# Who issues the 25 fills of the second adjacency matrix, and when

## The chip, the cores and the metric

The kernel runs on one core of one Trainium2 chip. The metric is the device time of one execution in microseconds (us). The engines are TensorE (PE; its weight loads are PEld), VectorE (DVE), ScalarE (ACT), GpSimd (POOL) and the sync engine (SP). A name with a q, as SPq, is the engine's sequencer, which also issues DMAs. SP and ACT have a DMA queue each (q1 and q10), GpSimd has q0, and all of them feed the same 16 DMA engines.

## The reference

The program is a chain of eight layers over 3125 nodes with 256 features: a graph layer and a feed-forward layer, four times. The change touches what the graph layers of level 1 and level 2 need, which are two weighted sums over the same 50,000 edges:

```python
# level 1 (four times)
norm = dinv[src] * dinv[dst]
out = segment_sum(h[src] * norm[:, None], dst) + b
# level 2 (twice)
norm = dis[row] * ew * dis[col]
out = segment_sum(h[row] * norm[:, None], col) + b
```

## The kernel before, in words

The kernel turns both sums into dense matrix products. It builds two matrices of 3200 rows by 3125 columns in HBM, one cell for each pair of nodes: `count_cells` holds how many edges join the pair (used by level 1), `weight_cells` the sum of their weights (used by level 2). Each is first filled, in 25 transfers of 128 rows (1562.5 KB each), from a stripe in SBUF, `edges_stripe`, that is zero but for a diagonal of ones. Then GpSimd adds the edges in, with scatters that add: one indirect DMA takes 128 cells.

The edges come in 392 columns of 128, in 49 windows of 8 columns (`NW = 49`, `WT = 8`). A scatter may not name a cell twice, and an add may not overtake another to the same cell. So edges of one window that fall into one cell are merged first, and GpSimd waits for all scatters of a window to land before it starts the next one.

Stages of PE, ACT, DVE and SP stand in one block and are separated by a barrier of those four engines. GpSimd isn't in these barriers: its work runs beside them, in its own order, and joins only at the end of the block. The order, with the lines:

- `cells_of_edges` (L493): ids of the cells, their digits, the gather of x. ACT issues the 25 fills of `count_cells` (L562).
- `cells_and_degrees` (L765): the merge. Class `Earlier` compares the edges of a window on PE and ACT, and DVE closes each window (L747). SP loads the digits, four transfers for a window, four windows ahead (`load`, L675): `sp.wait_ge(self.scored, WT * (w - self.RING + 1))` with `RING = 4`, so SP goes on to window w when window w - 4 is scored.
- `layer0_gnn` (from L992), `layer0_ffn`, `layer1_table` (L1341): the next layers; DVE waits at L1026 for all 25 fills of `weight_cells`. The last thing that SP issues there is `bins<-zeros` (L1349), 8704 KB of zeros to HBM.
- GpSimd beside all of it: `add_windows` (L464) calls `add_window` (L444) for each of the 49 windows. It waits for all 25 fills of `count_cells` once, then for the window's cells, then for the scatters of the window before; then it issues the eight scatters (L455) and, in windows 0 to 12, two fills of `weight_cells` (L460; one in window 12). After the last window it waits for all scatters.
- The block ends when all five engines are there (L2668), the semaphores are cleared, and the next block begins: `layer1_gnn` loads `count_cells` on SP (L1400), and GpSimd begins to scatter into `weight_cells` (L874).

Of the kernel before, what the change touches and what calls it, by code (L numbers as in the profile page):

```python
# [21 lines left out]
N = 3125  # L22
T = 25
P = N // T
# [12 lines left out]
NW = ET // WT  # L37
# [203 lines left out]
def linear(nc, g, tag, src, width, w_dram, bias_dram, nout, finish, prepare=None, turn=None, table=None,  # L241
# [10 lines left out]
    with ExitStack() as ctx:  # L252
# [17 lines left out]
        @block.sync  # L270
        def _(sp):
            column_loads = 0
            with nc.allow_non_contiguous_dma("a few hundred values"):
                for k, dram in enumerate((scale_dram, shift_dram)):
                    if dram is not None:
                        sp.dma_start(columns[0:rows, k, :], dram.rearrange("(k p) -> p k", p=rows)).then_inc(c_loaded, 16)
                        column_loads += 1
            if not in_sbuf:
                sp.dma_start(w[0:rows], w_dram.rearrange("(k p) n -> p k n", p=rows)).then_inc(w_loaded, 16)
            if bias is not None:  # L280
                sp.dma_start(bias[:, :], bias_dram.partition_broadcast(128)).then_inc(b_loaded, 16)
            for load in more_loads:
                load(sp)
            if table is not None:
                out = table[0].rearrange("(p t) d -> p t d", p=P)
                for t in range(0, T, G):

                    sp.wait_ge(put_away, t + G)
                    sp.dma_start(out[:, t:t + G, :], table[1][0:P, t:t + G, 0:nout]).then_inc(stored, 16)
                sp.wait_ge(stored, 16 * (T // G))  # L290
            for loads, loaded in ((column_loads, c_loaded), (not in_sbuf, w_loaded), (bias is not None, b_loaded)):
                if loads:
                    sp.wait_ge(loaded, 16 * loads)
# [143 lines left out]

FILLS = 2  # L440
FIRST_FILLS = 6


def add_window(nc, g, pool, w, e):  # L444


    rows = g.count_cells.rearrange("r (c a) -> (r c) a", a=1)
    if w == 0:
        pool.wait_ge(g.counts_filled, 16 * T)
    pool.wait_ge(g.cells_ready, w + 1)  # L450
    if w:

        pool.wait_ge(g.counts_added, 16 * WT * w)
    for t in range(w * WT, min((w + 1) * WT, EC + 1)):
        pool.indirect_dma_start(out=rows, out_offset=bass.IndirectOffsetOnAxis(ap=g.cell_row[:, t:t + 1], axis=0),  # L455
                                in_=g.cell_count[:, t:t + 1], in_offset=None, compute_op=ALU.add
                                ).then_inc(g.counts_added, 16)

    for j in range(FILLS * w, min(FILLS * (w + 1), T)):
        pool.dma_start(g.weight_cells[j * 128:(j + 1) * 128, :],  # L460
                       e.stripe[:, e.middle - j * P:e.middle - j * P + N]).then_inc(g.weights_filled, 16)


def add_windows(nc, g, e):  # L464


    @g.block.gpsimd
    def _(pool):
        for w in range(NW):
            add_window(nc, g, pool, w, e)  # L470
        pool.wait_ge(g.counts_added, 16 * (EC + 1))
# [182 lines left out]
class Earlier:  # L654
# [20 lines left out]
    def load(self, sp):  # L675
        own, other = self.e.side
        for w in range(NW):
            if w >= self.RING:
                sp.wait_ge(self.scored, WT * (w - self.RING + 1))
            tiles = slice(w * WT, (w + 1) * WT)  # L680
            j = w % self.RING
            for side, to, lo, hi in ((own, 0, 0, 5), (own, 5, 0, 3), (other, 0, 0, 3), (other, 5, 0, 5)):
                sp.dma_start(side[to:to + hi - lo, j, :],
                             self.g.digits_dram[lo:hi, tiles, :].rearrange("r t p -> r (t p)")).then_inc(self.loaded[j], 16)

    def start(self, dve):
        nc = self.nc
        nc.vector.memset(self.nothing[:, :], 0.0)
        nc.vector.tensor_copy(self.ident[:, :], self.g.ident[:, :])
        dve.wait_ge(self.e.later_ready, 1)  # L690
        nc.vector.tensor_copy(self.later[:, :], self.e.later[:, :])
        dve.drain().then_inc(self.copied, 1)
# [188 lines left out]
def aggregate(nc, g, tag, acc, table, width, weighted=False, field=0, loads=()):  # L881
# [4 lines left out]
    with ExitStack() as ctx:  # L886
# [11 lines left out]
        @block.sync  # L898
        def _(sp):
            for k, load in enumerate(loads):  # L900

                sp.wait_ge(multiplied, R + ST * (2 * k + 1) // (2 * len(loads)))
                load(sp)
# [1817 lines left out]
```

## Time and profile before

| | |
|---|---|
| median of 3 runs | 4455.87 us (4450.1 to 4464.65) |
| the profiled execution's own time | 4456.35 us |
| its span, first to last instruction | 4454.6 us |
| mean granted TensorE clock | 0.848 of full |
| PE busy | 3212.8 us, 72% |
| GpSimd busy | 2267.1 us, 51% |
| DVE busy | 1418.9 us, 32% |
| ACT busy | 882.3 us, 20% |

The shares are means over a program with many stages, so they don't say what a change in one stage is worth. The rows below are read from the first 1040 us of the span, where the change lies.

### The profile page before, as it was taken

How to read it: one execution, taken by the hardware profiler on the slowest of the kernel's cores; microseconds unless marked ns; L12 is line 12 of the kernel's file. 1: busy time of each engine (PE TensorE's matmuls, PEld its weight loads, DVE VectorE, ACT ScalarE, POOL GpSimd, SP SyncE). 2: the span in 40 equal slices, each digit the busy share in tenths (PEclk: the TensorE clock that was granted, in tenths of full speed). 3: DMA queues.
4: the chain of work that ended last, by engine and by line, in shares of the span. 5: the costliest groups of instructions: out<-in, count | busy, mean ns of one | idle time of the engine just before them, and what ended most of it. 6: DMA issues, size and time to landing. Idle time of an engine off the chain costs nothing. (4 is left out here: it accounts for less than half of the span.)

```text
span 4454.6 us, 56530 instructions
## 1 busy us (share of the span) xinstructions
PE 3212.8 (72%) x17915; PEld 2414.4 (54%) x17916; DVE 1418.9 (32%) x3628; ACT 882.3 (20%) x2505; POOL 2267.1 (51%) x1830
## 2 busy tenths in 40 slices
PE   0999855675999982893299999788785554553893
PEld 0555443565999982893288888645332222222562
DVE  3333365442531132012612111233433443442005
ACT  0666622120000000331301100133101111111220
POOL 5587777775666666665056665300006655552003
PEclk9999967787999995996699999789896676665996
DMA  8663212229999875797144334100343222232222
GB/s 338 236 182 77 9 2 5 11 16 282 274 294 266 257 190 156 195 244 182 25 150 145 131 118 146 44 0 0 118 140 89 84 81 80 80 75 70 92 95 68
DMA packets 368073, 562.48 MB, mean 126 GB/s; under 512 B 177053, under 2 KB 246493, under 8 KB 351584
## 3 DMA queue, kind: packets, MB, share of 16 engines
q1 hardware_dynamic: 201740, 393.74, 27.6%
q0 software_dynamic: 158320, 122.06, 14.8%
q10 hardware_dynamic: 7824, 44.20, 2.4%
q8 instruction: 114, 1.87, 0.2%
q14 instruction: 75, 0.61, 0.0%
HBM read 413.40 MB, written 145.88 MB: 126 GB/s over the span
## 5 line engine op out<-in xcount | busy, mean ns | idle before, releaser
L455 POOL DMA_INDIRECT count_cells<-cells_count,added_row x391 | 647.8, 1657 | 280.9 <-issue 119.5
L919 POOL DMA_INDIRECT g3g_got<-relations,g3g_idx x416 | 394.6, 948 | 765.2 <-ACT g3g_idx L912 645.1
L874 POOL DMA_INDIRECT weight_cells<-added_weight,added_row x391 | 609.3, 1558 | 318.5 <-DMA weight_cells<-added_weight,added_row 182.1
L1435 PE MATMUL g_acc<-XN,g_blocks 125*125 125x128 f32 x5000 | 567.3, 275 | 55.3 <-DMA g_blocks<-count_cells 52.7
L932 PE MATMUL g3g_pp<-g3g_got,g3g_hot 128*125 128x256 f32 x832 | 361.5, 563 | 325.6 <-DVE g3g_hot L943 153.2
L1435 PEld LDWEIGHTS g_acc<-XN,g_blocks 125*125 125x125 f32 x5000 | 559.2, 189 | 60.0 <-issue 52.9
L1748 PE MATMUL g_acc<-g_H,g_blocks 125*125 125x256 f32 x2500 | 552.4, 380 | 20.1 <-DMA g_blocks<-weight_cells 15.3
L1665 POOL DMA_INDIRECT slots_dram<-sort_rec,sort_row x392 | 379.4, 968 | 341.3 <-issue 120.1
L1748 PEld LDWEIGHTS g_acc<-g_H,g_blocks 125*125 125x125 f32 x2500 | 470.0, 188 | 94.7 <-issue 24.0
L932 PEld LDWEIGHTS g3g_pp<-g3g_got,g3g_hot 128*125 128x125 f32 x832 | 169.5, 255 | 518.1 <-DVE g3g_hot L943 271.3
L961 DVE TENSOR_TENSOR X<-X,g3g_pp 125x256 f32 x416 | 175.3, 421 | 362.8 <-issue 305.6
L723 ACT ACTIVATE same_same<-same_scores 128x128 bf16<-128x128 f32 (+7 forms) x392 | 255.1, 651 | 145.1 <-PE same_scores L712 127.2
L708 PE MATMUL same_scores<-edges_other,edges_own 11*128 11x512 bf16 (+2 forms) x490 | 206.9, 483 | 22.5 <-ACT same_same L723 21.5
L912 ACT CAST g3g_idx<-slots 128x1 int32 x416 | 79.4, 191 | 621.8 <-PE g3g_pp L932 409.3
L1792 DVE SCALAR_TENSOR_TENSOR g_tmp<-g_acc,dinv,g_b 125x256 f32<-125x256 f32 x50 | 24.2, 484 | 495.4 <-PE g_acc L1748 378.3
L2588 POOL DMA_INDIRECT f3y_Y<-results,f_back x25 | 36.0, 1440 | 275.2 <-PEq L86 267.8
L1875 PE MATMUL g_psO<-g_w,g_xT 128*125 128x512 f32 x400 | 173.7, 595 | 0.0
L943 DVE TENSOR_SCALAR g3g_hot<-iota,slots 128x125 f32<-128x125 f32 x424 | 127.6, 302 | 56.0 <-issue 42.7
L1456 ACT ACTIVATE g_uT<-g_psT 128x125 f32<-128x125 f32 (+1 forms) x75 | 20.6, 275 | 627.3 <-PE g_psT L1410 474.8
L2145 PE MATMUL f1e_pY<-w,XN 128*128 x512 | 123.0, 384 | 10.0 <-issue 10.0
L2123 PEld LDWEIGHTS f1e_pH<-XN,f1e_w 128*128 128x128 f32 x1040 | 128.2, 194 | 3.6 <-issue 0.2
L2123 PE MATMUL f1e_pH<-XN,f1e_w 128*128 128x128 f32 x1040 | 128.5, 278 | 0.0
(625 smaller groups left out, 4658.6 us busy)
## 6 DMA issues: line engine op xcount, KB each, us to landing
g_blocks<-count_cells SPq DMA_DIRECT2D x500, 312.5 KB
g_blocks<-weight_cells SPq DMA_DIRECT2D x50, 1562.5 KB
count_cells<-edges_stripe ACTq DMA_DIRECT2D x25, 1562.5 KB
weight_cells<-edges_stripe POOLq DMA_DIRECT2D x25, 1562.5 KB
f1e_w<-in_L_ffn_w SPq DMA_DIRECT2D x68, 512.0 KB
relations<-g_ys SPq DMA_DIRECT2D x25, 896.0 KB
f_w<-in_L_ffn_w SPq DMA_DIRECT2D x16, 1024.0 KB, 8.4
bins<-zeros SPq DMA_DIRECT2D x1, 8704.0 KB, 32.7
```

What stands on the lines that cost most here:

```text
L455: pool.indirect_dma_start(out=rows, out_offset=bass.IndirectOffsetOnAxis(ap=g.cell_row[:, t:t + 1], axis=0), in_=g.cell_count[:, t:t + 1], ...
L708: nc.tensor.matmul(self.scores[:, k % self.SCORES, lo:hi], own[:, j, n:n + 128], other[:, j, lo:hi], start=True, stop=True)
L723: self.nc.scalar.activation(self.same[:, k % self.SAME, 0:n], self.scores[:, k % self.SCORES, 0:n], ACT.Relu, accum_out=self.found[:, k:k ...
L874: pool.indirect_dma_start(out=rows, out_offset=bass.IndirectOffsetOnAxis(ap=g.cell_row[:, t:t + 1], axis=0), in_=g.cell_weight[:, t:t + 1] ...
L919: pool.indirect_dma_start(out=got[:, j, :], out_offset=None, in_=table[:, :], in_offset=bass.IndirectOffsetOnAxis(ap=idx[:, j:j + 1], axis ...
L932: nc.tensor.matmul(pp[0:P, j % BANKS, 0:width], hot[:, j, :], got[:, j, :], start=True, stop=True).then_inc(multiplied, 1)
L961: nc.vector.tensor_tensor(part, part, pp[0:P, j % BANKS, 0:width], ALU.add).then_inc(added, 1)
L1435: last = nc.tensor.matmul(acc[0:P, i % ACCS, 0:128], blocks[0:P, i % BLOCKS, t * P:(t + 1) * P], rhs[p][:, t, :], start=(t == 0), stop=(t ...
L1665: pool.indirect_dma_start(out=g.slots_dram[:, :], out_offset=bass.IndirectOffsetOnAxis(ap=self.row[:, c:c + 1], axis=0), in_=self.rec[:, c ...
L1748: last = nc.tensor.matmul(acc[0:P, i % 3, 0:D], blocks[0:P, i % BLOCKS, t * P:(t + 1) * P], H[p][0:P, t, :], start=(t == 0), stop=(t == T ...
L1875: last = nc.tensor.matmul(psO[0:P, c, :], xT[:, j, k, :], w[:, k, 2 * c:2 * c + 2, :].rearrange("p r n -> p (r n)"), start=(k == 0), stop= ...
L2123: last = nc.tensor.matmul(pH[:, j % 2, f * 128:(f + 1) * 128], w1[:, j % AHEAD, k, f * 128:(f + 1) * 128], xT[:, j % 2, k * 128:(k + 1) * ...
```

## The change

The two fills behind the scatters of windows 0 to 12 are removed from GpSimd. In their place SP issues one fill behind its digit loads of every odd window (1, 3, ..., 47) and one behind those of window 48, 25 in all. Data, sizes, the semaphore and who waits for it stay.

```diff
-FILLS = 2
@@ add_window
-    for j in range(FILLS * w, min(FILLS * (w + 1), T)):
-        pool.dma_start(g.weight_cells[j * 128:(j + 1) * 128, :],
-                       e.stripe[:, e.middle - j * P:e.middle - j * P + N]).then_inc(g.weights_filled, 16)
@@ Earlier.load
             for side, to, lo, hi in ((own, 0, 0, 5), (own, 5, 0, 3), (other, 0, 0, 3), (other, 5, 0, 5)):
                 sp.dma_start(side[to:to + hi - lo, j, :],
                              self.g.digits_dram[lo:hi, tiles, :].rearrange("r t p -> r (t p)")).then_inc(self.loaded[j], 16)
+            if w % 2 == 1 or w == NW - 1:
+                t = w // 2
+                sp.dma_start(self.g.weight_cells[t * 128:(t + 1) * 128, :],
+                             self.e.stripe[:, self.e.middle - t * P:self.e.middle - t * P + N]).then_inc(self.g.weights_filled, 16)
```

## Rows read from the trace of the kernel before

**Rows 1.** Where the engines reach the end of the first block (queue instructions, line L2668)

```profile
L2668 DVEq COMPARE_BRANCH  x1: 41/41/41, 999.4 to 999.4; - x1
L2668 POOLq COMPARE_BRANCH  x1: 41/41/41, 1031.3 to 1031.3; - x1
L2668 POOLq DRAIN  x1: 4467/4467/4467, 1031.5 to 1031.5; - x1
```

**Rows 2.** All scatters of L455: ns min/median/max, first and last start; what it waited for

```profile
L455 POOL DMA_INDIRECT count_cells<-cells_count,added_row x391: 1532/1541/7094, 147.2 to 1021.9; - x196
  issue: 119.5, 344
  DMA count_cells<-cells_count,added_row: 94.2, 46
```

**Rows 3.** Timeline of GpSimd: first scatter, boundary of windows 0 and 1 (start, us)

```profile
147.15 1.62 POOL L455 DMA_INDIRECT count_cells<-cells_count,added_row  x1 [67.21 <-DMA count_cells<-edges_stripe]
...
160.67 1.54 POOL L455 DMA_INDIRECT count_cells<-cells_count,added_row  x1 [0.30 <-issue]
161.66 1.77 POOL L460 DMA_DIRECT2D weight_cells<-edges_stripe  x2
164.45 1.65 POOL L455 DMA_INDIRECT count_cells<-cells_count,added_row  x1 [1.02 <-DMA count_cells<-cells_count,added_row]
```

**Rows 4.** First scatters of windows without a fill before them, in and after the merge

```profile
414.89 1.54 POOL L455 DMA_INDIRECT count_cells<-cells_count,added_row  x1 [2.08 <-DMA count_cells<-cells_count,added_row]
...
432.35 1.54 POOL L455 DMA_INDIRECT count_cells<-cells_count,added_row  x1 [2.10 <-DMA count_cells<-cells_count,added_row]
...
537.75 1.54 POOL L455 DMA_INDIRECT count_cells<-cells_count,added_row  x1 [2.06 <-DMA count_cells<-cells_count,added_row]
...
554.27 1.54 POOL L455 DMA_INDIRECT count_cells<-cells_count,added_row  x1 [2.06 <-DMA count_cells<-cells_count,added_row]
```

**Rows 5.** The moved issues: ns min/median/max, first and last start

```profile
L460 POOL DMA_DIRECT2D weight_cells<-edges_stripe x25: 1148/1161/1187, 161.7 to 377.0; - x25
```

**Rows 6.** Stretches: PE, PEld, DVE, ACT, POOL busy, clock, DMA share, GB/s

```profile
125.00:142.00 17.00, 16.06 (x144) 9.35 (x144) 5.79 (x25) 11.34 (x31) 0.00 (x0) 1.00 1.02 424
143.00:144.00 1.00, 1.00 (x7) 0.39 (x6) 0.91 (x3) 0.80 (x3) 0.00 (x0) 1.00 0.35 146
```

**Rows 7.** Timeline of SP: digit loads of windows 2, 3, 5, 7 and 9 (first half)

```profile
113.65 2.29 SPq L683 DMA_DIRECT2D edges_own<-digits_dram  x2
...
122.92 2.26 SPq L683 DMA_DIRECT2D edges_own<-digits_dram  x2
...
129.63 1.32 SPq L683 DMA_DIRECT2D edges_own<-digits_dram  x2
131.00 2.19 SPq L683 DMA_DIRECT2D edges_other<-digits_dram  x2
...
147.17 0.56 SPq L683 DMA_DIRECT2D edges_own<-digits_dram  x2
...
164.70 1.34 SPq L683 DMA_DIRECT2D edges_own<-digits_dram  x2
```

**Rows 8.** PE's first digits; SP's last digit loads, and its next stage

```profile
113.99 0.28 PE L710 MATMUL same_scores<-edges_other,edges_own 11*128 11x128 bf16 x1 [7.63 <-DMA edges_other<-digits_dram]
...
507.21 0.59 SPq L683 DMA_DIRECT2D edges_other<-digits_dram  x2
547.75 0.42 SPq L995 DMA_DIRECT2D l0g_w<-in_L_gnn_weight  x1
```

**Rows 9.** The end of the scatters and the zero fill (timeline; stretches; the wait of L874)

```profile
998.35 0.61 SPq L1349 DMA_DIRECT2D bins<-zeros  x1
...
1010.80 1.54 POOL L455 DMA_INDIRECT count_cells<-cells_count,added_row  x1 [6.29 <-DMA count_cells<-cells_count,added_row]
...
1021.87 1.54 POOL L455 DMA_INDIRECT count_cells<-cells_count,added_row  x1 [0.30 <-issue]
...
1026.00:1028.00 2.00, 0.00 (x0) 0.00 (x0) 0.00 (x0) 0.00 (x0) 0.00 (x0) 0.50 0.51 85
...
  DMA weight_cells<-added_weight,added_row: 182.1, 47
```

## The prediction

> **What bounds the kernel now.** I read first who arrives last at the end of the first block. DVE is there at 999.4 us, GpSimd only at 1031.3 us, and its drain takes another 4.5 us [rows 1]. So for the first 1036 us it is GpSimd's list of scatters that sets the time, and the other engines have 1031.3 - 999.4 = 32 us to spare. What comes after this block (the matrix products of level 1 start from the join) is shifted by whatever GpSimd is shifted, one for one.
>
> Second, GpSimd's own list. The 391 scatters run from 147.2 to 1021.9 us at 1.54 us each; between them lie 119.5 us of issue gaps and 94.2 us of waits for the scatters of the window before; ahead of the first stands a wait for the fills of `count_cells` [rows 2, 3]. It never waits for the merge. The list has two levers: when it starts, and how long a window takes.
>
> Third, the start. GpSimd's first scatter begins at 147.15 us, released by the fills of `count_cells` [rows 3]. Until 142 us the DMA engines are full, at 424 GB/s; in 143 to 144 us their share is down to 0.35 [rows 6]. I put the end of the bulk at 143.4 us. The start of the scatters is bound by DMA bandwidth, and nothing but bytes can move it.
>
> **What is removed: 25 issues on GpSimd.** Each takes 1.161 us, together 29 us [rows 5]. The reader might subtract these 29 us. But they stand inside a wait. The last scatter of window 0 starts at 160.67, the two fills occupy 161.66 to 163.43, GpSimd then is idle for another 1.02 us until the scatters have landed, and the next scatter starts at 164.45: 3.78 us from last scatter to next [rows 3]. Where there are no fills the same distance is 1.54 us for the scatter and 2.06 to 2.10 us idle, 3.6 us [rows 4]. So the landing of the scatters sets the boundary and the fills fill the wait. They cost at most the difference. Over the 12 boundaries that follow two fills, taking 0.1 us as the typical difference, that is 1.2 us gained; the bounds are 0 and 12 x 0.18 = 2.2 us. A whole window without fills takes 432.35 - 414.89 = 17.46 us [rows 4], one with them 164.45 - 147.15 = 17.30 us [rows 3]: no gain shows there either. If this cover were missing, the full 29 us would come back; that is a rival below.
>
> The Trainium skill, "DMA: Bandwidth & Descriptors", section "Anatomy of one DMA", puts some 2.0 us of fixed completion time on a small transfer from GpSimd. Behind a last scatter's 1.54 us, that would release the boundary after 3.5 us, an estimate by that page; the rows show 3.6 to 3.8, and by the page's figure the gain of the removal would be 12 x 0.25 = 3 us in place of 1.2.
>
> **What is added: fills while the first matrix is still being filled.** One fill is 1562.5 KB, 1.6 MB, which at the 424 GB/s of [rows 6] is 3.8 us of the full DMA bandwidth. In the kernel before no fill of `weight_cells` is issued ahead of 161.7 us [rows 5], that is, after the `count_cells` fills have ended. In the new order SP issues the first one behind the digits of window 1. The digits of window 2 go out at 113.65 us, those of window 4 at 122.92 us [rows 7]: so fill 0 leaves at about 114 us and fill 1 at about 124 us. SP passes to window 5 at 129.63 us, needs until 133.2 us for its four loads [rows 7], and then issues fill 2, with the delays of the earlier ones at about 135 us. Window 7 opens at 147.17 us, and its four loads take 1.2 us (two in 0.56) to 4 us, and then comes fill 3, at about 150 us.
>
> Bytes ahead of the end of `count_cells`: fills 0, 1 and 2 with certainty, 3 x 3.8 = 11.3 us. So the end moves from 143.4 to 154.7 us, and that is later than 150 us: fill 3 falls into it too. At 150 us there are 4.7 us of `count_cells` left; shared half and half with fill 3 (3.8 us) they end after another 4.7 + 3.8 us at most, at 158.5 us. If fill 3 is issued at 151.5 us, 3.2 us are left and end at 157.9 us. Window 9 opens only at 164.7 us [rows 7], so there is no fifth. The delay is 14.5 us, with bounds 11.3 and 15.1 us where the queues share the engines. The trace before can't show how two bulk queues share; a lower bound where ACT's queue keeps its place is nothing. I take sharing, as both streams have rows of the same size.
>
> The Trainium skill, "DMA: Bandwidth & Descriptors", section "Queues, rings and completion order", says that a DMA engine takes turns between its queues packet by packet. By that rule the fills and the first matrix share, the 14.5 us stand, and moving the issue to another engine wins no bandwidth; if one queue were drained first the term would be nothing.
>
> **On SP and the merge.** The fill is one more issue of at most 2 us on an engine that in window 7 needs 1.2 us for its loads [rows 7] and waits for PE the rest of an 8.8 us window. Digit loads queue behind fills on SP's queue: the digits of window 2, issued at about 116 us, then land at about 125 us (a fill at half the bandwidth takes 7.5 us). PE scores window 0 from 113.99 us [rows 8] and uses some 8.8 us per window, so it wants window 2 at 131 us, window 4 at 149 us. Each is in time. Should the merge still slip, the 32 us of room above cover it, and GpSimd, whose window takes 17.5 us, is far behind the merge. The last fill goes out after the last loads, at 508 us [rows 8]; the next stage begins at 547 us, and DVE asks for all of them later still.
>
> **During the scatters.** New fills come every 17.5 us until 508 us and occupy 3.8 us each. GpSimd's window has nearly the same period, so the phase counts. With a start near 161.7 us the last scatter of window 0 stands at 175.2 us. The fill of window 9 goes out at about 166 us and is through at 170 us. GpSimd's period is the longer one by 0.1 to 0.2 us, so the distance grows. Scatters in the middle of a window do not wait for landing. I price this at nothing; the other case is a rival.
>
> **At the end of the block.** The zero fill is issued at 998.35 us and is bulk traffic until 1026 us [rows 9]. It falls on two landings: the boundary before 1010.80 us shows an idle of 6.29 us in place of 2.1, 4.1 us more; and the last scatter, issued at 1021.87 us, is landed at 1031.3 us [rows 1, 9], 9.4 us in place of 3.7, so 5.7 us more. With a shift of some 12 us the last landing, at about 1040 us, falls behind the zero fill (5.7 us gained), the boundary before it stays in it, and the boundary one window of some 17 us earlier, near 986 us, comes to about 998 us and may lose 2 to 4 us. Net 2 to 4 us gained, I take 2.5. Last, the windows in the merge take 17.5 us and those after it 554.27 - 537.75 = 16.5 us [rows 4]; 14.5 us later means 0.8 window fewer in the merge: 0.8 us gained.
>
> **Sum.** 4456.35 (the profiled execution) + 14.5 - 1.2 - 2.5 - 0.8 = 4466.35 us, which is 10.0 us or 0.22% more. That execution lies 0.5 us above the median of the runs shown, so I say 4466 us. The own range of this case: start term 11.3 to 15.1, gains 2.0 to 8, so +3.3 to +13.1, and with some 3 us of noise 4457 to 4472.
>
> **Rivals.**
>
> A, the forecast: the start is delayed by the shared bandwidth, partly given back. Chance 0.62.
>
> B, the delay does not appear: ACT's queue keeps the bandwidth, or the issues of SP slip behind the end of `count_cells`. For it: no row shows two bulk queues at once. Then only the gaps of 1.2 us remain: 4455 us. It decides where the first scatter is still at 147 us. Chance 0.12.
>
> C, the issues on GpSimd do cost: faster. The boundary distance without fills would have to fall below the 3.6 us that the rows show. The full 29 us less the 14.5: 4456 - 29 + 14.5 - 1 = 4441 us. Against it speaks the 1.02 us of idle behind the fills. It decides if the landing takes less than the 2.8 us at which the fills end. Chance 0.07.
>
> D, collision: the fills run when a window's last scatters land, and stay there, as the two periods are almost equal. It decides if a fill is issued within 4 us ahead of a window's last scatter, which takes a start near 155 to 157 us. Price: while DMA was loaded, the boundary idles of L874 averaged 182.1/47 = 3.9 us [rows 9], 1.7 us above the quiet 2.1; the zero fill cost 4.1 us. Over 20 boundaries that is 34 to 82 us beside the 10: 4500 to 4550 us. Chance 0.09.
>
> E, GpSimd's list is shifted by more than the bytes: a stretched digit load or the merge holds it, or no landing escapes the zero fill: +15 to +25 us, 4471 to 4481 us. Chance 0.10.
>
> **Numbers.** Two medians of this kernel are told apart from about 0.3%, 13.4 us. Of A (its centre at +10) about one fifth lies above +13.4: 0.12, with D and E 0.31 slower. Faster takes C and a rest: 0.09. The remaining 0.60 is no change that can be told. Range 4447 to 4481 us: A, B and E are in, C and D are out with 0.16.
>
> **What would show it.** The first scatter of L455 at 158 to 163 us, its wait still on the fills of `count_cells` (A, E), or at 147 us (B). Full DMA share until about 158 us. Boundary distances of 3.6 to 3.7 us in windows 0 to 20 (A); well below 3.5 (C); above 5 (D). GpSimd's arrival at the end of the block at about 1041 us (A), with DVE still near 999 us. A later arrival of DVE by more than 30 us would make the whole argument wrong, as the merge would then be the bound.

## The result, and the profile after

| | before | changed |
|---|---|---|
| median of 20 runs each | 4459.74 us (4447.66 to 4474.61) | 4470.58 us (4452.7 to 4487.16) |
| ratio, with 95% interval | | 1.0025 [1.0013, 1.0036] |
| the profiled execution's own time | 4456.35 us | 4464.04 us |
| its span | 4454.6 us | 4462.3 us |

The changed kernel is 0.25% slower, 11 us (4459.74 x 0.0025; 6 to 16 us by the interval). On another chip, in the runs of the experiments, it was 4289.65 against 4277.3 us, ratio 1.0031 [1.0018, 1.0043]. That chip runs both kernels some 4% faster, but not the part that matters here: there the first scatter of the changed kernel begins at 161.82 us and GpSimd reaches the end of the block at 1048.6 us, on the first chip at 161.71 and 1048.6 us.

The scatters of the changed kernel, to be read against [rows 2] and the first line of [rows 3] (one instruction's summary, what it waited for, then its first instance in the timeline):

```profile
L454 POOL DMA_INDIRECT count_cells<-cells_count,added_row x391: 1539/1541/7590, 161.7 to 1043.7; - x196
  issue: 127.3, 345
  DMA count_cells<-cells_count,added_row: 101.0, 42
  DMA count_cells<-edges_stripe: 81.7, 1
...
161.71 1.62 POOL L454 DMA_INDIRECT count_cells<-cells_count,added_row  x1 [81.70 <-DMA count_cells<-edges_stripe]
```

The reader is to see that the list starts 161.71 - 147.15 = 14.6 us later and that its wait is for the same thing as before, the fills of `count_cells`, 81.7 us of it in place of 67.2.

The fills as SP issues them (timeline), and the DMA engines in the stretches around the new end of the `count_cells` fills (last three columns: TensorE clock, DMA share, GB/s), against [rows 6, 7]:

```profile
113.14 1.09 SPq L682 DMA_DIRECT2D weight_cells<-edges_stripe  x1
...
123.37 1.10 SPq L682 DMA_DIRECT2D weight_cells<-edges_stripe  x1
...
133.90 1.11 SPq L682 DMA_DIRECT2D weight_cells<-edges_stripe  x1
...
150.99 1.11 SPq L682 DMA_DIRECT2D weight_cells<-edges_stripe  x1
...
142.00:157.00 15.00, 14.40 (x122) 7.87 (x122) 5.21 (x17) 10.75 (x27) 0.00 (x0) 1.00 1.00 417
157.00:158.00 1.00, 0.67 (x12) 0.47 (x13) 0.00 (x0) 0.67 (x5) 0.00 (x0) 1.00 0.61 229
158.00:161.00 3.00, 3.00 (x26) 1.77 (x23) 2.49 (x10) 1.48 (x5) 0.00 (x0) 1.00 0.23 90
```

Four fills go out before the engines fall idle, and the bandwidth stays at 417 GB/s until 157 us, where it had dropped in 142 to 144 us before.

The end of the block, against [rows 1, 9] (arrivals at the block's end, then the last landings in the timeline):

```profile
L2667 DVEq COMPARE_BRANCH  x1: 41/41/41, 1003.1 to 1003.1; - x1
L2667 POOLq COMPARE_BRANCH  x1: 41/41/41, 1048.6 to 1048.6; - x1
L2667 POOLq DRAIN  x1: 3437/3437/3437, 1048.7 to 1048.7; - x1
```

```profile
1015.29 1.54 POOL L454 DMA_INDIRECT count_cells<-cells_count,added_row  x1 [6.32 <-DMA count_cells<-cells_count,added_row]
...
1032.60 1.54 POOL L454 DMA_INDIRECT count_cells<-cells_count,added_row  x1 [2.85 <-DMA count_cells<-cells_count,added_row]
...
1043.67 1.54 POOL L454 DMA_INDIRECT count_cells<-cells_count,added_row  x1 [0.30 <-issue]
```

GpSimd is still the last, by 45 us, and arrives 17.3 us later than before. The last scatter lands 1048.6 - 1043.67 = 4.9 us after it starts, where it took 9.4 us in the zero fill before; the zero fill now hits the boundary before 1015.29 us.

The ledger of the list, from all 391 scatters of each trace (the last window has seven). A boundary is the place between two windows, where GpSimd waits for the landing. "Extra duration" is what the scatters took above 1.54 us each, "boundary idle" the idle at the boundaries above the quiet 2.1 us, "mid-window idle" the idle inside windows above the usual 0.3 us:

| us | before | changed | difference |
|---|---|---|---|
| first scatter starts | 147.15 | 161.71 | +14.6 |
| extra duration | 45.3 | 45.5 | +0.2 |
| boundary idle | 14.1 | 16.4 | +2.3 |
| mid-window idle | 9.5 | 14.3 | +4.8 |
| last scatter starts | 1021.87 | 1043.67 | +21.8 |
| its landing, to GpSimd's arrival | 9.4 | 4.9 | -4.5 |
| arrival | 1031.3 | 1048.6 | +17.3 |

The next block starts when GpSimd's drain is over: at 1036.0 us before (a drain of 4.5 us), at 1052.2 us after (3.4 us), so the join moved by 16.2 us.

### The profile page after: what moved, and what is told of

It reads as the page before. It is cut to its first block and busy times, and to the rows that moved or that the text cites. A ratio compares the mean times of both kernels' runs of the same rounds, so it can differ in the third digit from the quotient of the medians.

```text
span 4462.3 us, 56530 instructions
## 1 busy us (share of the span) xinstructions
PE 3206.1 (72%) x17915; PEld 2411.5 (54%) x17916; DVE 1418.3 (32%) x3628; ACT 883.0 (20%) x2505; POOL 2254.7 (51%) x1805
## 5 line engine op out<-in xcount | busy, mean ns | idle before, releaser
L1747 PE MATMUL g_acc<-g_H,g_blocks 125*125 125x256 f32 x2500 | 551.2, 380 | 17.5 <-DMA g_blocks<-weight_cells 15.0
```

Source lines behind the costliest of these rows:

```text
L1747: last = nc.tensor.matmul(acc[0:P, i % 3, 0:D], blocks[0:P, i % BLOCKS, t * P:(t + 1) * P], H[p][0:P, t, :], start=(t == 0), stop=(t == T ...
```

## The experiments

Each kernel below is described behind the table. Its ratio is to runs of the kernel before on the same chip, and is not the quotient of the medians. e1_late, e3_first_four, e4_one_per_window and z1_zero_early shared one chip (kernel before: median 4453.35 us). The others ran on three more: e5, e6, e7 and e8 on one (4276.64 us), the changed kernel again, e9 and z2 on one (4277.3 us), e10 on one (4276.96 us). The other columns come from one trace of each kernel; the kernel before was traced on the chip of the result alone.

| run | first scatter | last scatter | boundary idle | mid-window idle | GpSimd's arrival | ratio [95%] |
|---|---|---|---|---|---|---|
| before | 147.15 | 1021.87 | 14.1 | 9.5 | 1031.3 | 1 |
| changed, again | 161.82 | 1043.24 | 16.1 | 15.8 | 1048.6 | 1.0031 [1.0018, 1.0043] |
| e1_late | 146.97 | 1039.71 | 26.2 | 13.9 | 1045.1 | 1.0014 [0.9998, 1.0030] |
| e3_first_four | 160.90 | 1035.07 | 16.3 | 7.9 | 1040.2 | 1.0026 [1.0009, 1.0043] |
| e4_one_per_window | 173.79 | 1052.59 | 18.4 | 11.3 | 1057.6 | 1.0065 [1.0040, 1.0091] |
| z1_zero_early | 146.61 | 1026.86 | 17.1 | 9.7 | 1032.3 | 0.9997 [0.9981, 1.0012] |
| e5_locked | 146.94 | 1029.61 | 17.3 | 14.4 | 1034.8 | 1.0003 [0.9994, 1.0012] |
| e8_single_late | 146.49 | 1030.29 | 16.9 | 14.1 | 1035.3 | 1.0005 [0.9996, 1.0014] |
| e6_fifty_fills | 147.70 | 1042.38 | 27.8 | 14.4 | 1047.6 | 1.0034 [1.0022, 1.0046] |
| e7_pool_one_per_window | 147.15 | 1015.33 | 12.1 | 6.2 | 1025.8 | 1.0001 [0.9992, 1.0010] |
| e9_x_late | 137.40 | 1020.05 | 19.1 | 9.2 | 1024.9 | 0.9977 [0.9968, 0.9986] |
| z2_x_late_zero_early | 138.20 | 1026.60 | 21.9 | 10.0 | 1031.9 | 0.9989 [0.9980, 0.9998] |
| e10_x_locked | 137.68 | 1015.02 | 15.1 | 11.3 | 1022.0 | 0.9974 [0.9963, 0.9984] |

**The changed kernel again** (run label a2_changed_again). No edit.

> The changed kernel once more, beside the others on one chip: theory 1 says ratio 1.002 to 1.003, and the first scatter again at 161.7 us (161.0 to 162.4).

As expected, with the first scatter at 161.82 us and the ratio at the edge of the band.

**Only the early four moved to SP** (e3_first_four). The kernel before, with

```diff
-    for j in range(FILLS * w, min(FILLS * (w + 1), T)):
+    for j in range(4 + FILLS * w, min(4 + FILLS * (w + 1), T)):
@@ Earlier.load
+            if w in (1, 3, 5, 7):
+                t = w // 2
+                sp.dma_start(self.g.weight_cells[t * 128:(t + 1) * 128, :], ...).then_inc(self.g.first_filled, 16)
```

> One part alone: SP issues only fills 0 to 3 (behind windows 1, 3, 5, 7), the other 21 stay on GpSimd, two per window from window 0 on. Theory 1: first scatter at 161.7 us as in the changed kernel, time 10 to 14 us above the kernel before, ratio 1.0022 to 1.0032. Rival 1: the later 21 fills made the price, so this one is within 3 us of the kernel before, ratio 0.9995 to 1.0007.

The first scatter is at 160.90 us and the ratio is 1.0026, as large as the whole price of the change. The other 21 fills add nothing to the time that these runs can tell. In the trace they do make a difference: GpSimd arrives 8.4 us earlier than in the changed kernel (1048.6 - 1040.2), and 6.4 us of that is mid-window idle.

**The early four taken out of the changed kernel** (e8_single_late).

```diff
-            if w % 2 == 1 or w == NW - 1:
-                t = w // 2
+            singles = [*range(9, 40, 2), *range(40, NW)]
+            if w in singles:
+                t = singles.index(w)
```

> The changed kernel with only its early fills moved: SP issues one fill behind each odd window from 9 to 39 and one behind each window from 40 to 48, none before. Theory 1 (the first four fills set the price): first scatter at 147 us, list end 1022 to 1030 us, as single fills drift through one or two landings at 1 to 4 us each; time 0 to 6 us above the kernel before, ratio 1.000 to 1.0013. Rival 1 (fills from SP in the merge are the price): list end at 1035 us or later, ratio 1.002 or more.

The first scatter is back at 146.49 us and the time at 1.0005, inside the expected band, while the changed kernel stands at 1.0031 on a chip of the same speed; the two intervals don't meet. The list ends at 1030.3 us, the edge of what theory 1 allowed: 8.4 us later than before, though it started no later. Of these, 4.6 us are mid-window idle (14.1 us in place of 9.5) and 2.8 us idle at boundaries. The last landing, clear of the zero fill, gives 4.4 us back, so GpSimd arrives 4 us later.

**A first attempt at the same, in bursts of two fills** (e1_late).

```diff
-            if w % 2 == 1 or w == NW - 1:
-                t = w // 2
+            for t in range(w - 9, min(w - 7, T)) if w % 2 == 1 and w >= 9 else ():
```

> As the changed kernel, but SP issues no fill of weight_cells before window 9 (two behind each odd window from 9 to 31, one behind 33). Theory 1 (the fills cost bandwidth ahead of the first scatter, and nothing else of size): the first scatter is back at 147 us, GpSimd reaches the end of the block at 1027 to 1033 us, the time is 1 to 4 us below the kernel before (ratio 0.9990 to 1.0000). Rival 1 (fills from SP anywhere in the merge meet landings of scatters, and that is the price): at least 5 us of the 11 stay, ratio 1.001 or more. Rival 2 (the issues on GpSimd were worth their 29 us): ratio 0.994.

A miss for theory 1 in its plain form. The start is back at 146.97 us, but the arrival is not: 1045.1 us. The trace shows one place (GpSimd, then SP):

```profile
282.78 2.14 POOL L454 DMA_INDIRECT count_cells<-cells_count,added_row  x1 [5.93 <-issue]
...
288.91 1.54 POOL L454 DMA_INDIRECT count_cells<-cells_count,added_row  x1 [0.30 <-issue]
299.63 1.54 POOL L454 DMA_INDIRECT count_cells<-cells_count,added_row  x1 [9.18 <-DMA count_cells<-cells_count,added_row]
...
319.35 1.63 POOL L454 DMA_INDIRECT count_cells<-cells_count,added_row  x1 [5.05 <-DMA count_cells<-cells_count,added_row]
```

```profile
289.29 0.82 SPq L681 DMA_DIRECT2D weight_cells<-edges_stripe  x2
```

A mid-window stall of 5.93 us stands before it; then the pair of fills leaves 0.4 us after the last scatter of window 7 and its landing takes 7.1 us more than the quiet 2.1 of idle; the next boundary loses 2.9 us. So the collision of rival D is real, at this one place. It did not befall the changed kernel, but it befell this one.

**The same, with SP held until a landing is over** (e5_locked): e1_late with

```diff
+            if w % 2 == 1 and 9 <= w <= 33:
+                sp.wait_ge(self.g.counts_added, 16 * WT * ((w - 7) // 2))
```

> As e1_late (SP issues no fill before window 9, two behind odd windows 9 to 31, one behind 33), but SP first waits until the scatters of GpSimd's window (w - 7) / 2 - 1 have landed, so that a pair of fills always starts right behind a landing. Theory 1 with the collision as the cause of what e1_late lost: the first scatter at 147 us, extra idle at GpSimd's boundaries back from 26 to 14 to 17 us, the list ends at 1020 to 1027 us, time 0 to 6 us below the kernel before (ratio 0.9987 to 1.0003). Rival (what e1_late lost is a price of the fills coming from SP, whenever they come): the list ends near 1038 us as there, ratio 1.001 or more.

The boundary idle is 17.3 us in place of 26.2 and the ratio 1.0003. The list ends at 1029.6 us, 2.6 us later than theory 1 said, again with 14.4 us of mid-window idle. So phase, not the issuing engine, made most of what e1_late lost. GpSimd still arrives 3.5 us later than before.

**More fills ahead of the start** (e4_one_per_window): `for t in (w,) if w < T else ():` in place of the condition, one fill behind every window 0 to 24.

> The suspected cost enlarged: SP issues one fill behind the digits of every window 0 to 24, so that 10 or 11 instead of 4 lie ahead of the end of the count_cells fills. Theory 1: first scatter at 147.15 + 10 or 11 x 3.8 = 185 to 189 us, time 30 to 42 us above the kernel before, ratio 1.007 to 1.009. If ACT's queue gets less than half, the start is the same (the bytes are all ahead of it). Rival 1: no growth of the start beyond 165 us, the price in the boundaries of windows 0 to 4.

Right in kind, too high in size for the start. It moves by 173.79 - 147.15 = 26.6 us, which is 7 fills of 3.8 us and not 10 or 11. The issues show why (timeline of SP):

```profile
136.99 1.10 SPq L681 DMA_DIRECT2D weight_cells<-edges_stripe  x1
...
148.22 1.13 SPq L681 DMA_DIRECT2D weight_cells<-edges_stripe  x1
159.64 1.13 SPq L681 DMA_DIRECT2D weight_cells<-edges_stripe  x1
170.59 1.08 SPq L681 DMA_DIRECT2D weight_cells<-edges_stripe  x1
```

They come 11 us apart and not 8.8: the digits stand behind the fills in SP's queue, PE waits for them five times in 110 to 180 us (21.4 us in all, against 7.6 us once before) and falls behind (7.2 of 10 us busy from 150 to 160 us, 9.5 before), and SP, which waits for PE, issues later. Nine fills were issued ahead of 171.6 us, when the last bytes of `count_cells` had moved, and by then SP's queue had moved 12.3 MB, 7.7 fills. The arrival moves by 26.3 us and the time by 0.65%, 29 us, with only four runs (18 to 41 us by the interval): arrival follows the start one for one, and the time agrees with that.

**Fifty issues on GpSimd** (e6_fifty_fills): behind each fill the same once more, into a spare tensor.

```diff
+        pool.dma_start(g.spare_cells[j * 128:(j + 1) * 128, :],
+                       e.stripe[:, e.middle - j * P:e.middle - j * P + N]).then_inc(g.weights_filled, 16)
```

> The kernel before, with every fill on GpSimd issued twice, the second time into a spare tensor: four issues behind the scatters of windows 0 to 11 instead of two, two in window 12. Theory (two issues lie inside the wait for the landing, four do not): distance from last scatter to next 5.3 to 5.8 us instead of 3.78 in these windows, list end 18 to 24 us later, ratio 1.004 to 1.0055. Rival (issues on GpSimd cost their full 1.16 us from the first one on): 2 x 1.16 us per window more, 29 us, ratio 1.0065. Rival (they cost nothing at all): ratio 1.000.

Between the theories. The list ends 20.5 us later, inside the 18 to 24 us, but the time grows by 14.5 us (4276.64 x 0.0034; 9 to 20 us by the interval), less than the 17 to 24 us that the expected ratio means, and not 29. The boundary of windows 0 and 1:

```profile
161.12 1.55 POOL L455 DMA_INDIRECT count_cells<-cells_count,added_row  x1 [0.30 <-issue]
162.10 1.20 POOL L460 DMA_DIRECT2D weight_cells<-edges_stripe  x1
162.70 1.18 POOL L462 DMA_DIRECT2D spare_cells<-edges_stripe  x1
163.27 1.13 POOL L460 DMA_DIRECT2D weight_cells<-edges_stripe  x1
163.79 1.12 POOL L462 DMA_DIRECT2D spare_cells<-edges_stripe  x1
165.22 1.65 POOL L455 DMA_INDIRECT count_cells<-cells_count,added_row  x1 [0.30 <-issue]
```

With four issues the idle of 1.02 us [rows 3] is down to the plain issue gap of 0.30 us and the distance is 165.22 - 161.12 = 4.10 us. Four overlapping issues take 2.8 us, not 4 x 1.16. At half of the 12 boundaries the distance was near 4.1, at the others 4.6 to 6.0 us. The cover holds two issues and nearly four. But this kernel also moves 25 fills more, and at the slow boundaries GpSimd waits for the landing and not for its issues, so it doesn't tell the price of an issue from that of the added bytes.

**One issue per window on GpSimd** (e7_pool_one_per_window): `FILLS = 1`.

> The kernel before, with one fill per window on GpSimd in windows 0 to 24 instead of two in 0 to 12. If two issues are hidden in the wait, one is too: distance from last scatter to next 3.6 to 3.7 us in windows 0 to 12, list end within 3 us of the kernel before, ratio 0.9993 to 1.0007. If the last 0.1 us per window of the pair counts, this run shows it: 1 us lower. If issues cost wherever they stand, nothing changes either, as there are 25 in both; then e6_fifty_fills decides.

1.0001. The boundary idle of the list is 2 us less than with two, the mid-window idle 3.3 us less. GpSimd arrives 5.5 us earlier, and nothing of it stands out in the time; its interval, -3.4 to +4.3 us, leaves no room for the 5.5 us, and the runs don't show where they went. Spreading the same 25 issues over twice as many windows gains nothing that can be measured.

**Fewer bytes ahead of the start** (e9_x_late). The kernel before, with the load of x into X taken from the first stage and issued by SP in the merge:

```diff
@@ Earlier.load
+            if w == 36:
+                sp.wait_ge(self.g.counts_added, 16 * WT * 14)
+                for lo, hi in STRIPS:
+                    sp.dma_start(self.g.X[lo:hi], ...).then_inc(self.e.x_loaded, 16)
```

> The kernel before, with 3.2 MB of other traffic taken out of the stretch ahead of the first scatter: the load of x into X (needed first near 658 us) is issued by SP in window 36 of the merge, behind the landing of GpSimd's window 13. Theory 1 (bytes ahead of the end of the count_cells fills set the start, at 3.8 us per 1.6 MB): first scatter 7 to 8 us earlier, at 139 to 140 us, list end 4 to 10 us earlier, ratio 0.998 to 0.999. Rival (the start hangs on the order of the fills themselves, or x was hidden): start at 146 to 147 us, ratio 1.000.

The start is 9.8 us earlier (147.15 - 137.40), somewhat more than the bytes say, and the ratio 0.9977. The list ends only 1.8 us earlier, not 4 to 10. It lost 7 us again at one boundary, 10.82 us from last scatter to next, where x was in flight:

```profile
402.09 1.54 POOL L455 DMA_INDIRECT count_cells<-cells_count,added_row  x1 [0.30 <-issue]
412.91 1.54 POOL L455 DMA_INDIRECT count_cells<-cells_count,added_row  x1 [9.27 <-DMA count_cells<-cells_count,added_row]
```

**The same, behind the next landing** (e10_x_locked): `w == 37` and a wait for 15 windows.

> As e9_x_late, but x is loaded one window later and only once GpSimd's window 14 has landed, so that its 12 us of traffic lie between two landings. If the 7 us that the landing of window 14 lost in e9_x_late (10.8 in place of 3.8 us) came from that traffic, the boundary of windows 14 and 15 is under 5 us again, the list ends 5 to 8 us earlier than there, ratio 0.996 to 0.9975. If the loss only moves to another boundary or is unrelated, the ratio stays at 0.9977.

```profile
403.95 1.54 POOL L455 DMA_INDIRECT count_cells<-cells_count,added_row  x1 [0.30 <-issue]
407.66 1.54 POOL L455 DMA_INDIRECT count_cells<-cells_count,added_row  x1 [2.17 <-DMA count_cells<-cells_count,added_row]
```

The boundary is back to 3.7 us and the list ends 5.0 us earlier. The ratio of 0.9974 is the best of all, faster than both kernels, but it can't be told from that of e9_x_late.

**The zero fill out of the way** (z1_zero_early). The kernel before, without SP's zero fill at the end of the block, and in `add_window`

```diff
+    for lo in range(0, 68, 11)[max(0, 2 * (w - 13)):max(0, 2 * (w - 12))]:
+        hi = min(lo + 11, 68)
+        pool.dma_start(g.bins.rearrange("(p r) d -> p (r d)", p=128)[:, lo * D:hi * D],
+                       e.stripe[:, 0:(hi - lo) * D]).then_inc(g.cleared, 16)
```

> The kernel before (fills on GpSimd), with the 8704 KB of zeros not issued by SP at the end of the block but by GpSimd in 7 pieces right behind the last scatters of windows 13 to 16. Theory: the zero fill costs two landings 4.1 and 5.7 us, so GpSimd reaches the end of the block at 1021 to 1023 us instead of 1031.3, and the time is some 10 us lower, ratio 0.9978. Rival: the pieces cost their issue time of 1.2 us each on GpSimd (8 us), ratio 0.9995; or the end of the block is bound elsewhere, ratio 1.000.

A miss: 0.9997. The two landings were freed, as the trace shows at the boundary into the last window:

```profile
1012.04 1.54 POOL L455 DMA_INDIRECT count_cells<-cells_count,added_row  x1 [0.30 <-issue]
1015.79 1.54 POOL L455 DMA_INDIRECT count_cells<-cells_count,added_row  x1 [2.21 <-DMA count_cells<-cells_count,added_row]
```

But the list had lost the time by then. Its dearest boundary, beside DVE's long operation:

```profile
660.86 6.61 POOL L455 DMA_INDIRECT count_cells<-cells_count,added_row  x1 [0.30 <-issue]
672.78 1.54 POOL L455 DMA_INDIRECT count_cells<-cells_count,added_row  x1 [5.31 <-DMA count_cells<-cells_count,added_row]
```

```profile
659.23 6.83 DVE L1056 TENSOR_TENSOR X<-X,l0g_XT 125x6400 f32<-125x6400 f32 x1
```

A scatter issued while that operation runs takes up to 7 us. If it is the last of its window, the landing comes late as well, 11.9 us from last scatter to next in place of 3.7; 3.2 us of that is idle above the quiet 2.1 us, while the next stage's weights are loaded (214 GB/s from 669 to 671 us). In the kernel before the same operation met the first scatter of a window, for 4.8 us. Which scatter it meets is a matter of phase.

**Both** (z2_x_late_zero_early): the edits of e9_x_late and z1_zero_early.

> Both: x loaded in the merge, and the zeros written by GpSimd in 7 pieces behind windows 13 to 16. Theory: start at 139 to 140 us, no landing slowed at the end of the block (boundary of window 47 at 3.7 us, final landing under 6 us); GpSimd's arrival 8 to 17 us earlier than in the kernel before, ratio 0.9965 to 0.9985. If what z1_zero_early lost in the middle of the list comes again, only the start remains: 0.998 to 0.9995.

0.9989, no better than e9_x_late alone; the intervals overlap. GpSimd arrives at 1031.9 us, not earlier than in the kernel before. That misses the first band and falls into the second: the early zeros lose again what they free.

## Why the prediction was right

**What bounds.** Right. GpSimd was the last at the block's end in every run, by 20 to 47 us. In e4_one_per_window, where DVE too came 13 us later, DVE was still there first.

**The start.** Forecast +14.5 us, measured +14.6, and both neighbours in dose agree in sign and kind: e3_first_four +13.8, e4_one_per_window +26.6, e9_x_late -9.8. The fills went out at 113.1, 123.4, 133.9 and 151.0 us, forecast 114, 124, 135 and 150. The forecast assumed that SP's and ACT's fills share the engines, and the trace shows it: from 141 to 144 us SP's queue moved 0.51 MB and ACT's 0.74 MB, together 415 GB/s, where ACT's alone had 424 before. Before the last bytes of ACT's fills had moved, at 160.4 us (146.2 before), SP's queue had moved 6.4 MB, four whole fills. The Trainium skill, "DMA: Bandwidth & Descriptors", section "Issuing engines are not separate DMA queues", says that DMAs of different engines run on the same 16 DMA engines and interleave, so that another issuer saves only issue time. The trace agrees with that: the start moved by 14.6 us.

**The removed issues.** Forecast 1.2 us gained; the traces show none. The first twelve boundaries of the kernel before, with two issues in each, took 3.65 to 3.85 us from last scatter to next, on average 3.74 us, but for one of 5.14 us; the first six of the changed kernel, with none, took 3.61 to 3.81 us, on average 3.73. The 3.6 us that the prediction took for the quiet distance is the low end. Rival C, 29 us, falls: e5_locked and e8_single_late have all 25 issues off GpSimd and its start at 147 us, and are not faster. The prediction also put the gain at 3 us from the 2.0 us that the Trainium skill, "DMA: Bandwidth & Descriptors", section "Anatomy of one DMA", gives for such a transfer. The boundaries don't show that gain: their quiet distance is 3.7 us and not 3.5.

**The collision.** Priced at nothing for the changed kernel, and none came: no fill was issued within 6.5 us ahead of a window's last scatter, and the idle at the boundaries rose by 2.3 us in all. As a mechanism it is real (e1_late, e9_x_late), at 7 us a time. That it stayed away was partly luck. The prediction said that the distance from a fill to the next last scatter would grow. It shrank, from 8.7 us in window 0 to 7.0 us in window 6, as GpSimd's first six windows took 17.15 us on average and SP's two 17.5; then a stall of 4.79 us on GpSimd set it to 11.5 us. Nor did all boundaries stand at the forecast 3.6 to 3.7 us: of the first 20, twelve took 3.6 to 3.8 us and eight 4.2 to 5.9 us. In e8_single_late a boundary of 4.5 us stands even before the first fill, so the fills need not be their cause, which stays open.

**The zero fill.** Forecast 2 to 4 us gained. The last landing gave back 4.5 us, the boundaries of windows 46 and 47 took 0.7 us less together (12.25 against 12.93 us), so 5.2 us. Right in kind, and too small by half. The last landing gave less than the forecast 5.7 us, as clear of the zero fill the way from the last scatter to the arrival is 4.9 us and not the 3.7 us from scatter to scatter. The boundary before it, forecast to stay slow, came clear too, as the shift was larger than forecast. The 0.8 us for fewer windows in the merge doesn't show: the extra duration of the scatters did not fall (+0.2 us).

**What was missing.** The mid-window idle rose by 4.8 us. It consists of a few stalls, for which the profile names no releaser ("issue"). The changed kernel has six of them where the kernel before has five, which makes some 1.5 us. Its longest, 4.79 us with a fill issued 1.2 us ahead of it, at 288.89 us, stands against 3.26 us before, 1.5 us more; and one of 3.85 us at 671 us, while weights of the next stage are loaded and no fill is under way, stands against 1.8 to 1.9 us, 2 us more. The traces tell two things about these stalls. First, their place is fixed by the program: in all kernels without fills on GpSimd the six stand before the same six scatters. Second, their length isn't. The stall before the 61st scatter, in the changed kernel and in e4_one_per_window:

```profile
294.87 1.54 POOL L454 DMA_INDIRECT count_cells<-cells_count,added_row  x1 [4.79 <-issue]
...
308.44 1.54 POOL L454 DMA_INDIRECT count_cells<-cells_count,added_row  x1 [1.86 <-issue]
```

It lasts 4.8 to 5.9 us where the DMA engines move 156 to 294 GB/s during it (both runs of the changed kernel, e1_late, e5_locked), and 1.9 us where they move less than 20 (e4_one_per_window, e8_single_late). In all the traces the stalls under 2.2 us have nearly no such traffic, with two exceptions of 1.9 us at 285 and 295 GB/s, and 15 of the 19 longer ones have it, 52 GB/s or more. Traffic in flight, of whatever origin, goes with the long stalls; what GpSimd waits for in them stays open. e3_first_four has 7.9 us of mid-window idle, and e6_fifty_fills, whose fills come from GpSimd, has 14.4 us, so it isn't a price of SP as the issuer.

**The sum.** Forecast +10.0 us, measured +11 (4459.74 x 0.0025, with the interval 6 to 16), and 13 on the second chip (4277.3 x 0.0031). The mechanism and its main term, the start, are right; that the total comes within 1 us is partly luck. GpSimd's arrival was forecast at about 1041 us and came at 1048.6 us: it moved by 17.3 us and the join by 16.2 us, more than the time did, and as much as rival E (+15 to +25 us) said of a list shifted by more than the bytes. The terms that made the difference are the mid-window idle of 4.8 us, which the prediction didn't have, 3.0 us at the boundaries ahead of the zero fill and 2.0 us of gains that did not come, against 2.7 us more given back by the zero fill.

From the join on, the profiled execution was 8.5 us shorter than before: 2.3 us in the second block (1120.3 and 1118.0 us), 5.6 us in the third (1864.9 and 1859.3 us), the rest behind it. The change touches neither, and on one chip the third block took between 1859.7 and 1879.4 us in the traces of e1_late, e3_first_four, e4_one_per_window and z1_zero_early. So I read the 8.5 us as scatter of single executions; it isn't shown. Over all experiments, each set against the join of the one trace of the kernel before, the time followed the join one for one within some 7 us: e3_first_four +7.7 and +12, e4_one_per_window +25.2 and +29, e6_fifty_fills +16.2 and +14.5, but e1_late +12.8 and +6, e7_pool_one_per_window -6.3 and 0.

## What to carry to other kernels

A DMA that is moved to an idle engine still needs the same DMA engines: look first at what they do at the new time of issue, and at who waits for the last byte there. Issues that stand inside a wait for a landing can be free where they are, as two per window were here, and they keep their distance from the next landing; a queue that another engine paces has neither. If a start is bound by bytes, take bytes away from ahead of it: that was worth 0.23% here, where the change cost 0.25%.

## What the runs showed of the hardware

- From the last scatter of a window (128 four-byte cells) to the first of the next it takes 3.6 to 3.9 us in quiet, and took 10.7 to 11.2 us where a pair of 1.6 MB fills, or 3.2 MB of loads, was in flight (e1_late, e9_x_late, z2_x_late_zero_early).
- Issues of plain DMAs on GpSimd overlap: 1.1 to 1.2 us each, but only 0.5 to 0.6 us apart when four follow one another (e6_fifty_fills).
- A scatter's 1.54 us on GpSimd grew to 4.7 to 8.2 us when it met one of DVE's two tensor-tensor operations of 6.8 us on 125x6400 elements (all traces).
- Small loads behind bulk stores in one queue can slow the stage that issues the stores: in e4_one_per_window the distance of SP's issues grew from 8.8 to 11 us.
- GpSimd's long list of scatters has stalls of 1.7 to 2.2 us at places that the program fixes, and of 2.7 to 7.2 us mostly where bulk traffic is in flight; their cause is open.
